# The first experts' second offset: from a TensorE product in PSUM to a GpSimd addition in SBUF

## The chip, the cores and the metric

The kernel runs on one core of a Trainium2 chip. A core has engines with instruction queues of their own that meet only at semaphores: TensorE (PE, products and transposes into PSUM), VectorE (DVE), ScalarE (ACT), GpSimd (POOL) and SyncE (SP, which here only issues DMAs). The metric is device microseconds (us) of one execution, less is better. In the profile PEld stands for TensorE's loading of the stationary operand.

## What is computed

The whole program is four layers on 12,500 nodes of 256 features: a graph layer, a layer of 8 experts, a second graph layer, and attention with 4 experts. The change touches the layer of 8 experts alone:

```python
# L0_ffn, E = 8 experts, C slots for each, D = 256, F = 1024
buf  = zeros((E, C, D)).at[idx, pos_safe].set(x)              # rows sent to their expert
hmid = relu(einsum('ecd,edf->ecf', buf, w1) + b1[:, None, :])
ybuf = einsum('ecf,efd->ecd', hmid, w2) + b2[:, None, :]      # b2: the second offset
```

`b2` has one row of 256 numbers for each expert, added to each row of that expert's result.

## The kernel before

`program` calls one function for each stage, with a barrier of all engines between them. `run_experts` is the stage of the 8 experts. Two jobs that share no data run in it side by side.

**The experts** are TensorE's job. The 8 x 2048 slots are cut into 32 blocks (`NB`) of 512 rows, four blocks for an expert. For block `g` TensorE makes 8 tiles of the hidden layer (`hid_ps`, L1568), each from two products, ScalarE applies ReLU and the first offset to each (L1607), and then TensorE makes four result tiles of 128 x 256 (`y_ps`, index `q`, L1587), each a sum over 8 products in PSUM. Ahead of these 8 stands one product of the first three partitions, `ones_bf` by `b2_bf` (L1583): its three rows are three bf16 parts of `b2` that add up to its float32 value, and it writes the offset to the tile first (`start=True`). ScalarE copies each tile to the buffer `y` in SBUF (L1614, two buffers) and raises `y_done`. SP stores a block when its four tiles are copied (`store`, L1522). Between the result tiles 0 and 2 of a block TensorE also transposes the next block's rows (`turn_rows`, L1550).

**A sort** of edge records is VectorE's job, with help. It is a bitonic network on keys `key` and a payload `pay`, both 128 x 2048 float32. Its steps are `flip` (a change of sign, L374), `swap` (compare and exchange at a distance) and `turn` (a transposition by TensorE). A swap is five instructions of VectorE in a chain, each waiting for the one before: a mask `is_gt` (L384), `min` (L385), `max` (L386), and two predicated copies that move the payload (L390, L391). The first predicated copy overwrites what the second needs, so GpSimd copies half of the payload to `spare` first (`sort_holds`, L404): the copy waits for the step before (`w.chain`), and VectorE waits for the copy (`w.held`) ahead of L390. In this stage run 105 swaps, 14 turns and 7 flips, and GpSimd does nothing but the 105 copies.

In a turn TensorE transposes eight pieces of 128 x 512 (`sort_turn`, L415) and VectorE copies each back from PSUM (L379), so a turn needs both engines at the same time: TensorE waits there for VectorE's chain, VectorE for TensorE's transposes. Where the turns stand in TensorE's queue is fixed by `turn_places`. It counts 6 slots for a block (two in the hidden layer, one behind each result tile, 192 in all), gives each sort step a cost (flip 1, turn 9, swap 7, 868 in all), and places a turn at the slot that the cost spent so far reaches, with `FILL = 0.9` of the slots for the whole sort. The 14 turns stand at slots 0, 8, 20, 30, 42, 54, 65, 78, 90, 104, 116, 132, 144 and 161. Behind the last turn come 7 more swaps.

Ahead of the sort VectorE splits `b2` into its three parts (`split_offsets`, ten instructions on three partitions, L1620 to L1632). When the sort is done VectorE writes the records and counts them, TensorE adds up the counts at the end of the last block's hidden layer (`plan_sums`, L182), VectorE makes the plan's columns of the sums, and SP stores them (`plan_store`, L188) and the last block of results.

Of the kernel before, what the change touches and what calls it, by code (L numbers as in the profile page):

```python
# [5 lines left out]
F32, I32, BF16, U16 = mybir.dt.float32, mybir.dt.int32, mybir.dt.bfloat16, mybir.dt.uint16  # L6
ALU, ACT, AX = mybir.AluOpType, mybir.ActivationFunctionType, mybir.AxisListType

P = 128
N, D = 12500, 256  # L10
# [103 lines left out]
def bc(ap, n, axis=2):  # L114

    a = ap.unsqueeze(axis)
    shape = list(a.shape)
    shape[axis] = n
    return a.to_broadcast(shape)
# [1343 lines left out]
def turn_places(w, first, last, slots):  # L1463


    cost = lambda step, by: {"flip": 1, "turn": 9, "swap": 7}[step]
    total = sum(cost(*w.steps[i]) for i in range(first, last))
    places, spent = {}, 0
    for i in range(first, last):
        if w.steps[i][0] == "turn":  # L1470
            places.setdefault(min(slots - 1, int(spent * FILL / total * slots)), []).append(i)
        spent += cost(*w.steps[i])
    return places


FILL = 0.9


def run_experts(nc, k, xbuf, w1, b1, w2, b2, ybuf, w, first, plan, dest):
# [7 lines left out]
    NB = EXPERTS * BLOCKS  # L1487
    last = len(w.steps)
    with Stage(nc) as s:
        w1s = [s.sb(f"w1s{n}", [P, 2, HID], F32) for n in range(2)]  # L1490
        w2s = [s.sb(f"w2s{n}", [P, FC, D], F32) for n in range(2)]
        b1s = [s.sb(f"b1s{n}", [P, FC], F32) for n in range(2)]
        b2_all, b2_left = s.sb("b2_all", [3, EXPERTS, D], F32), s.sb("b2_left", [3, EXPERTS, D], F32)
        b2_part, b2_bf = s.sb("b2_part", [3, EXPERTS, D], F32), s.sb("b2_bf", [3, EXPERTS, D], BF16)
        ones_bf = s.sb("ones_bf", [3, P], BF16)
        x = [s.sb(f"x{n}", [P, 4, D], F32) for n in range(2)]
        xt = [s.sb(f"xt{n}", [P, 2, W], F32) for n in range(2)]
        hid = [s.sb(f"hid{n}", [P, FC, W], F32) for n in range(2)]
        y = [s.sb(f"y{n}", [P, 4, D], F32) for n in range(2)]
        xt_ps = s.ps("xt_ps", [P, W])  # L1500
        hid_ps = [s.ps(f"hid_ps{n}", [P, W]) for n in range(HB)]
        y_ps = [s.ps(f"y_ps{n}", [P, 512]) for n in range(2)]
        sort_ps = [s.ps(f"sort_ps{h}", [P, 512])[:, :] for h in range(2)]
        r = Records(s, w, plan, sort_ps[0])
        weights, x_loaded, y_stored = ([s.sem(f"{n}{h}") for h in range(2)] for n in ("weights", "x_loaded", "y_stored"))
        turned, xt_done, hid_mult, hid_done, y_mult, y_done, b2_in, split, b2_done = (s.sem(n) for n in (
            "turned", "xt_done", "hid_mult", "hid_done", "y_mult", "y_done", "b2_in", "split", "b2_done"))
        places = turn_places(w, first, last, NB * 6)
        with nc.Block() as block:
            @block.sync  # L1510
            def _(sp):
                def load_weights(e):
                    n = e % 2
                    if e >= 2:
                        sp.wait_ge(y_mult, (e - 1) * BLOCKS * 4)
                    sp.dma_start(w1s[n][:, :, :], w1[e, :, :].rearrange("(c p) f -> p c f", p=P)).then_inc(weights[n], 16)
                    sp.dma_start(w2s[n][:, :, :], w2[e, :, :].rearrange("(c p) d -> p c d", p=P)).then_inc(weights[n], 16)
                    sp.dma_start(b1s[n][:, :], b1[e, :].rearrange("(c p) -> p c", p=P), allow_slow_non_contiguous=True).then_inc(weights[n], 16)

                def store(g):  # L1520
                    sp.wait_ge(y_done, g * 4 + 4)
                    sp.dma_start(yv[g, :, :, :], y[g % 2][:, :, :]).then_inc(y_stored[g % 2], 16)  # L1522

                for g in range(NB):
                    if g >= 2:
                        sp.wait_ge(turned, (g - 1) * 2)
                    sp.dma_start(x[g % 2][:, :, :], xv[g, :, :, :]).then_inc(x_loaded[g % 2], 16)
                    if g == 0:
                        sp.dma_start(b2_all[:, :, :], b2.unsqueeze(0).to_broadcast([3, EXPERTS, D])).then_inc(b2_in, 16)
                        load_weights(0)  # L1530
                    if g % BLOCKS == 1 and g < NB - BLOCKS:
                        load_weights(g // BLOCKS + 1)
                    if g >= 2:
                        store(g - 2)
                store(NB - 2)
                records_stored(sp, w, r, dest)
                store(NB - 1)
                sp.wait_ge(r.columns.kept, 16)
                sp.wait_ge(r.stored, 16)
                for h in range(2):  # L1540
                    sp.wait_ge(y_stored[h], 16 * (NB // 2))

            @block.tensor
            def _(pe):
# [14 lines left out]
                for g in range(NB):  # L1559
                    n, wide = g // BLOCKS % 2, slots_of(g)  # L1560
                    pe.wait_ge(xt_done, g * 2 + 2)
                    pe.wait_ge(weights[n], 48 * (g // BLOCKS // 2 + 1))
                    for fc in range(FC):
                        h = g * FC + fc
                        if h >= HB:
                            pe.wait_ge(hid_done, h - HB + 1)
                        for c in range(2):
                            ins = nc.tensor.matmul(hid_ps[h % HB][:, 0:wide], w1s[n][:, c, fc * P:(fc + 1) * P], xt[g % 2][:, c, 0:wide], start=c == 0, stop=c == 1)  # L1568
                        ins.then_inc(hid_mult, 1)
                        if fc % 4 == 3:  # L1570
                            sort_turns(g * 6 + fc // 4)
                    if g == NB - 1:
                        plan_sums(nc, pe, k, r.columns)
                    for q in range(4):
                        if q % 2 == 0 and g < NB - 1:
                            turn_rows(g + 1, q // 2)
                        m = g * 4 + q
                        if m >= 2:
                            pe.wait_ge(y_done, m - 1)
                        out = y_ps[q % 2][:, 0:D]  # L1580
                        if m == 0:
                            pe.wait_ge(b2_done, 1)
                        nc.tensor.matmul(out, ones_bf[:, :], b2_bf[:, g // BLOCKS, :], start=True, stop=False)  # L1583
                        for fc in range(FC):
                            if q == 0:
                                pe.wait_ge(hid_done, g * FC + fc + 1)
                            ins = nc.tensor.matmul(out, hid[g % 2][:, fc, q * P:(q + 1) * P], w2s[n][:, fc, :], start=False, stop=fc == FC - 1)  # L1587
                        ins.then_inc(y_mult, 1)
                        sort_turns(g * 6 + 2 + q)

            @block.scalar
            def _(act):
# [6 lines left out]
                for g in range(NB):  # L1599
# [8 lines left out]
                    for q in range(4):  # L1608
                        if q % 2 == 0 and g < NB - 1:
                            copy_turned(g + 1, q // 2)  # L1610
                        act.wait_ge(y_mult, g * 4 + q + 1)
                        if q == 0 and g >= 2:
                            act.wait_ge(y_stored[g % 2], 16 * (g // 2))
                        nc.scalar.activation(y[g % 2][:, q, :], y_ps[q % 2][:, 0:D], ACT.Copy).then_inc(y_done, 1)  # L1614

            @block.vector
            def _(dve):
                def split_offsets(link):

                    link(nc.vector.memset(ones_bf[:, :], 1.0))  # L1620
                    dve.wait_ge(b2_in, 16)
                    for row in range(3):
                        own = k.ident[0:3, row:row + 1]
                        link(nc.vector.tensor_scalar(b2_left[:, :, :].bitcast(I32), b2_all[:, :, :].bitcast(I32), 16, 16,
                                                     ALU.logical_shift_right, ALU.logical_shift_left))
                        if row < 2:
                            link(nc.vector.tensor_tensor(b2_all[:, :, :], b2_all[:, :, :], b2_left[:, :, :], ALU.subtract))
                        if row == 0:
                            link(nc.vector.tensor_scalar(b2_part[:, :, :], b2_left[:, :, :], own, None, ALU.mult))
                        else:  # L1630
                            link(nc.vector.scalar_tensor_tensor(b2_part[:, :, :], b2_left[:, :, :], own, b2_part[:, :, :], ALU.mult, ALU.add))
                    link(nc.vector.tensor_copy(b2_bf[:, :, :], b2_part[:, :, :]))  # L1632
                    dve.sem_inc(b2_done, 1)

                split_offsets(Chain(dve, split))
                sort_on_vector(nc, dve, w, first, last, sort_ps)
                records_on_vector(nc, dve, k, w, r)

            @block.gpsimd
            def _(pool):  # L1640
                sort_holds(pool, nc.gpsimd.tensor_copy, w, first, last)


def normalize_nodes(nc, k, sums, params, x_old, x_left, f_turned, w, width, result):
# [852 lines left out]
```

## Time and profile before

| | us |
|---|---|
| median of 3 runs | 9306.64 |
| lowest and highest | 9304.74, 9342.89 |
| the profiled execution, its own time | 9387.91 |
| its span, first to last instruction | 9386.1 |

| in the profiled execution | |
|---|---|
| the stage `run_experts` | 2775 to 3843 us |
| PE busy, whole span | 5874.7 us (63%) |
| POOL busy | 4973.1 us (53%) |
| DVE busy | 4494.3 us (48%) |
| ACT busy | 3781.8 us (40%) |

The shares over the whole span are means over ten stages with different limits. What the change is worth has to be read in its stage, from four views: the busy times of the engines in stretches, the groups of instructions by line, the waits, and the instructions in order of time. The profiled execution is 81 us longer than the median; the difference is not in one stage's rows, and its own durations are used against its own span.

### The profile page before, as it was taken

Reading aid. Unit: us, or ns where it says so; the run is one execution under the profiler, and the core shown is the slowest. Engines: PE = TensorE matmul, PEld = TensorE weight load, DVE = VectorE, ACT = ScalarE, POOL = GpSimd, SP = SyncE. Lnnn points to the kernel's source line nnn. Section 1 sums busy time; section 2 is a strip of 40 time slices with the busy share of each in tenths; the row PEclk is TensorE's granted clock in tenths of the full one; section 3 lists DMA queues with packets and bytes.
Section 4 is the critical chain, followed back from the end, with each engine's and each line's share of the span. In section 5 each row is a group of like instructions: output and inputs, shape, how many; then the busy total and the mean of one; then the engine's idle time right before and its main releaser. Section 6 shows DMA issues by size and latency. Waiting matters only on the chain. (4 is left out here: it accounts for less than half of the span.)

```text
span 9386.1 us, 89224 instructions
## 1 busy us (share of the span) xinstructions
PE 5874.7 (63%) x19881; PEld 3964.3 (42%) x19881; DVE 4494.3 (48%) x8790; ACT 3781.8 (40%) x9693; POOL 4973.1 (53%) x4762
## 2 busy tenths in 40 slices
PE   5455555555569999655555555555647677676755
PEld 4333333333356666333443333333624444444444
DVE  4444555545569999564544444444711111111125
ACT  5555555555552222444554554555401111111113
POOL 4666666666542222546666666666454544454532
PEclk8666667777659999876776676676568878787878
DMA  5333333333321111542332222232321111111126
GB/s 147 99 99 100 98 100 101 95 90 89 100 97 41 50 54 41 142 150 87 89 89 84 86 83 83 84 89 81 130 56 43 41 41 41 42 42 42 44 74 253
DMA packets 500454, 797.42 MB, mean 85 GB/s; under 512 B 123070, under 2 KB 365355, under 8 KB 499851
## 3 DMA queue, kind: packets, MB, share of 16 engines
q0 software_dynamic: 200256, 453.47, 18.0%
q1 hardware_dynamic: 299696, 338.23, 11.2%
q8 instruction: 196, 3.21, 0.1%
q14 instruction: 306, 2.51, 0.1%
HBM read 595.60 MB, written 197.30 MB: 84 GB/s over the span
## 5 line engine op out<-in xcount | busy, mean ns | idle before, releaser
L1017 PE MATMUL part<-rows,spread 128*128 x6656 | 2441.4, 523 | 2142.5 <-issue 1124.7
L1017 PEld LDWEIGHTS part<-rows,spread 128*128 128x128 f32 x6656 | 1624.7, 261 | 2905.8 <-issue 2631.6
L974 DVE TENSOR_TENSOR agg<-agg,part 128x257 f32 (+1 forms) x3328 | 1405.6, 422 | 2401.1 <-issue 866.3
L957 POOL DMA_INDIRECT rows<-h,row x1563 | 1555.7, 995 | 876.9 <-issue 439.9
L957 POOL DMA_INDIRECT rows<-f,row x1563 | 1555.2, 995 | 767.3 <-issue 456.8
L1041 ACT ACTIVATE spread<-iota,place 128x128 f32<-128x128 f32 x3328 | 1020.2, 392 | 2186.2 <-PE part L1017 1057.9
L1921 POOL DMA_INDIRECT rows<-gat,src x1122 | 1062.0, 947 | 1097.4 <-DVEq L2108 764.5
L1996 PE MATMUL y_ps<-agg,hid 128*128 128x256 f32 x3136 | 888.0, 423 | 658.4 <-issue 653.1
L1996 PEld LDWEIGHTS y_ps<-agg,hid 128*128 128x128 f32 x3136 | 661.1, 212 | 906.0 <-issue 821.1
L1047 ACT ACTIVATE spread<-spread,weight 128x128 f32<-128x128 f32 x3328 | 1021.2, 391 | 14.5 <-ACT spread L1043 0.9
L2126 DVE TENSOR_TENSOR y_all<-y_ps,b 128x512 f32<-128x512 f32 x196 | 135.5, 692 | 1792.1 <-DMA h<-res 1046.2
L2029 ACT ACTIVATE hid<-hid_ps,b 128x512 f32<-128x512 f32 (+1 forms) x400 | 261.5, 679 | 1684.8 <-DMA own<-sorted_e 1214.1
L1985 PE MATMUL hid_ps<-agg,w 128*128 128x512 f32 (+1 forms) x1600 | 707.9, 594 | 40.3 <-issue 28.3
L404 POOL COPY spare<-pay 128x1024 f32<-128x1024 f32 x105 | 222.5, 2119 | 735.3 <-DVE pay L391 505.6
L1043 ACT ACTIVATE spread<-spread,ones 128x1024 f32<-128x1024 f32 x416 | 478.6, 1150 | 38.9 <-remote 21.3
L1587 PE MATMUL y_ps<-w2s,hid 128*128 128x256 f32 x2048 | 476.2, 386 | 0.0
L1985 PEld LDWEIGHTS hid_ps<-agg,w 128*128 128x128 f32 x1600 | 312.0, 195 | 382.7 <-issue 356.3
L1568 PE MATMUL hid_ps<-xt,w1s 128*128 128x512 f32 (+1 forms) x1024 | 427.7, 574 | 3.5 <-DMA b1s<-in_L_ffn_b 3.5
L385 DVE TENSOR_TENSOR key<-key 128x1024 f32<-128x1024 f32 (+1 forms) x342 | 414.1, 1211 | 6.1
L1587 PEld LDWEIGHTS y_ps<-w2s,hid 128*128 128x128 f32 x2048 | 378.5, 190 | 61.7
L386 DVE TENSOR_TENSOR key<-key 128x1024 f32<-128x1024 f32 (+1 forms) x342 | 337.5, 987 | 11.8
L1607 ACT ACTIVATE hid<-hid_ps,b1s 128x512 f32<-128x512 f32 (+1 forms) x256 | 171.2, 669 | 329.0 <-PE hid_ps L1568 329.0
(393 smaller groups left out, 6035.2 us busy)
## 6 DMA issues: line engine op xcount, KB each, us to landing
expert_rows<-y_all SPq DMA_DIRECT2D x196, 256.0 KB
made<-expert_rows SPq DMA_DIRECT2D x49, 1024.0 KB
x<-x SPq DMA_DIRECT2D x42, 896.0 KB
rows<-f,row POOLq DMA_INDIRECT x1563
rows<-h,row POOLq DMA_INDIRECT x1563
rows<-gat,src POOLq DMA_INDIRECT x1122
xbuf<-zero SPq DMA_DIRECT2D x128, 128.0 KB
x<-xbuf SPq DMA_DIRECT2D x32, 512.0 KB
```

Of the source, the lines that this page charges most:

```text
L385: link(nc.vector.tensor_tensor(b[:, :, 0, :], a[:, :, 0, :], a[:, :, 1, :], ALU.min))
L957: pool.indirect_dma_start(out=rows[:, u, 0:D], out_offset=None, in_=table, in_offset=bass.IndirectOffsetOnAxis(ap=q.row[:, i:i + 1], axis= ...
L974: nc.vector.tensor_tensor(sum_t, sum_t, part[:, p % NB, 0:WIDE], ALU.add).then_inc(added, 1)
L1017: nc.tensor.matmul(part[:, p % NB, 0:WIDE], spread[:, p % (2 * BANKS), :], row_p, start=True, stop=True).then_inc(multiplied, 1)
L1041: nc.scalar.activation(spread[:, p % (2 * BANKS), :], k.iota[:, :], ACT.Square, bias=q.place[:, p:p + 1]).then_inc(squared, 1)
L1043: nc.scalar.activation(spread[:, h, :], spread[:, h, :], ACT.Relu, scale=-1.0, bias=k.ones[:, 0:1]).then_inc(marked, 1)
L1047: nc.scalar.activation(spread[:, p % (2 * BANKS), :], spread[:, p % (2 * BANKS), :], ACT.Copy, scale=q.weight[:, p:p + 1]).then_inc(spread ...
L1568: ins = nc.tensor.matmul(hid_ps[h % HB][:, 0:wide], w1s[n][:, c, fc * P:(fc + 1) * P], xt[g % 2][:, c, 0:wide], start=c == 0, stop=c == 1)
L1587: ins = nc.tensor.matmul(out, hid[g % 2][:, fc, q * P:(q + 1) * P], w2s[n][:, fc, :], start=False, stop=fc == FC - 1)
L1921: pool.indirect_dma_start(out=rows[b % 3][:, j, :], out_offset=None, in_=table, in_offset=at(src[:, b * B + j:b * B + j + 1])).then_inc(ga ...
L1985: ins = nc.tensor.matmul(hid_ps[m % HB][:, 0:cols_n], w1[:, e, d, fc * P:(fc + 1) * P], ft[n // GEXP % 2][:, d, 0:cols_n], start=d == 0, s ...
L1996: ins = nc.tensor.matmul(y_ps[m % 2][:, q, :], hid[n % 2][:, fc, at:at + P], w2[:, n % GEXP, fc, :], start=fc == 0, stop=fc == FC - 1)
```

## The change

GpSimd adds the offset, to the four result tiles of a block at once, in SBUF. In full:

- `b2` is loaded for all 128 partitions (`b2_p`, 128 x 8 x 256 float32) in the place of the load for three partitions, in the same place of SP's queue, ahead of the first weights. The split into three parts on VectorE goes, and with it `ones_bf`, `b2_bf` and `b2_done`.
- The product L1583 goes, 128 of them. The first of the 8 products of a tile starts the sum.
- GpSimd's `add(g)` waits until the four tiles of block `g` are copied and adds the expert's row to 128 x 1024 numbers, in place. There are 32 such additions. `turn_places` returns for each step of the sort the slot it reaches (`reached`), and `add(g)` stands ahead of the first payload copy whose step reaches slot `(g + 1) * 6`; four are left behind the last copy.
- The store of a block waits for its addition (`offset`) in the place of `y_done`.
- `y` has four buffers in the place of two.

```diff
@@ run_experts
-        b2_all, b2_left = s.sb("b2_all", [3, EXPERTS, D], F32), s.sb("b2_left", [3, EXPERTS, D], F32)
-        b2_part, b2_bf = s.sb("b2_part", [3, EXPERTS, D], F32), s.sb("b2_bf", [3, EXPERTS, D], BF16)
-        ones_bf = s.sb("ones_bf", [3, P], BF16)
+        b2_p = s.sb("b2_p", [P, EXPERTS, D], F32)
+        YB = 4
...
@@ sync
-                    sp.wait_ge(y_done, g * 4 + 4)
-                    sp.dma_start(yv[g, :, :, :], y[g % 2][:, :, :]).then_inc(y_stored[g % 2], 16)
+                    sp.wait_ge(offset, g + 1)
+                    sp.dma_start(yv[g, :, :, :], y[g % YB][:, :, :]).then_inc(y_stored[g % YB], 16)
...
-                        sp.dma_start(b2_all[:, :, :], b2.unsqueeze(0).to_broadcast([3, EXPERTS, D])).then_inc(b2_in, 16)
+                        sp.dma_start(b2_p[:, :, :], b2.unsqueeze(0).to_broadcast([P, EXPERTS, D])).then_inc(b2_in, 16)
@@ tensor
-                        if m == 0:
-                            pe.wait_ge(b2_done, 1)
-                        nc.tensor.matmul(out, ones_bf[:, :], b2_bf[:, g // BLOCKS, :], start=True, stop=False)
...
-                            ins = nc.tensor.matmul(out, hid[g % 2][:, fc, q * P:(q + 1) * P], w2s[n][:, fc, :], start=False, stop=fc == FC - 1)
+                            ins = nc.tensor.matmul(out, hid[g % 2][:, fc, q * P:(q + 1) * P], w2s[n][:, fc, :], start=fc == 0, stop=fc == FC - 1)
@@ vector
-                split_offsets(Chain(dve, split))
@@ gpsimd
-                sort_holds(pool, nc.gpsimd.tensor_copy, w, first, last)
+                def add(g):
+                    pool.wait_ge(y_done, g * 4 + 4)
+                    rows = y[g % YB][:, :, :]
+                    nc.gpsimd.tensor_tensor(rows, rows, bc(b2_p[:, g // BLOCKS, :], 4, 1), ALU.add).then_inc(offset, 1)
+
+                pool.wait_ge(b2_in, 16)
+                g = 0
+                for i in range(first, last):
+                    while g < NB - 1 and (g + 1) * 6 <= reached[i]:
+                        add(g)
+                        g += 1
+                    sort_holds(pool, nc.gpsimd.tensor_copy, w, i, i + 1)
+                for g in range(g, NB):
+                    add(g)
```

On GpSimd, at the start of `run_experts` (L404 is the payload copy, L1624 the addition):

```order
-L1639 UNCONDITIONAL_BRANCH
-L404 COPY spare<-pay 128x1024 x105
-L1509 UNCONDITIONAL_BRANCH
+L1619 UNCONDITIONAL_BRANCH
+L404 COPY spare<-pay 128x1024 x3
+L1624 TENSOR_TENSOR y_57979<-y_57979,b_p 128x1024
+L404 COPY spare<-pay 128x1024 x3
+L1624 TENSOR_TENSOR y_57980<-y_57980,b_p 128x1024
+L404 COPY spare<-pay 128x1024 x5
+L1624 TENSOR_TENSOR y_57981<-y_57981,b_p 128x1024
+L404 COPY spare<-pay 128x1024 x3
```

The one unbroken row of 105 copies is cut: an addition stands behind every three to five copies, 28 in all, and four more behind the last copy.

On TensorE, the first block's result tiles, before:

```order
L1568 MATMUL hid_ps_57987<-xt_57979,w1s_57966 128x512 x2
L1550 MATMUL xt_ps<-ident,x_57978 128x128 x4
L1583 MATMUL y_ps_57989<-b_bf,ones_bf 128x256
L1587 MATMUL y_ps_57989<-w2s_57968,hid_57981 128x256 x8
L1583 MATMUL y_ps_57990<-b_bf,ones_bf 128x256
L1587 MATMUL y_ps_57990<-w2s_57968,hid_57981 128x256 x8
L1550 MATMUL xt_ps<-ident,x_57978 128x128 x4
```

and with the change:

```order
L1569 MATMUL hid_ps_57985<-xt_57975,w1s_57966 128x512 x2
L1551 MATMUL xt_ps<-ident,x_57974 128x128 x4
L1585 MATMUL y_ps_57987<-w2s_57968,hid_57977 128x256 x8
L1585 MATMUL y_ps_57988<-w2s_57968,hid_57977 128x256 x8
L1551 MATMUL xt_ps<-ident,x_57974 128x128 x4
```

Only the product L1583 ahead of each result tile is gone. The order of all that remains, the turns' slots among it, is the same.

## Rows read from the trace of the kernel before

**Rows 1.** Busy time by stretch (us, PE, PEld, DVE, ACT, POOL, granted clock, DMA):

```profile
2900.00:3000.00 100.00, 98.25 (x388) 64.16 (x387) 95.15 (x72) 24.16 (x42) 23.24 (x11) 1.00 0.16 53
...
3154.00:3161.00 7.00, 6.59 (x30) 5.11 (x29) 4.62 (x7) 0.00 (x0) 0.00 (x0) 0.51 0.06 22
```

**Rows 2.** Waits of the stage (who, for whom: us in total, times, longest):

```profile
DVE first L209 <- PE sort_ps L182: 58.5, 1, 58.5
DVE key L379 <- PE sort_ps L415: 24.9, 16, 3.7
...
PE sort_ps L415 <- DVE key L374: 6.2, 2, 3.7
```

**Rows 3.** Groups by line and shape, the stage (busy us, mean ns, idle before):

```profile
L404 POOL COPY spare<-pay 128x1024 f32<-128x1024 f32 x105 | 222.5, 2119 | 735.3 <-DVE pay L391 505.6 <-DVE pay L379 229.6
L385 DVE TENSOR_TENSOR key<-key 128x1024 f32<-128x1024 f32 x105 | 206.3, 1964 | 3.6
...
L391 DVE COPY_PREDICATED pay<-mask,spare 128x1024 f32<-128x1024 uint16 x105 | 167.1, 1591 | 3.6
...
L384 DVE TENSOR_TENSOR mask<-key 128x1024 uint16<-128x1024 f32 x105 | 128.7, 1225 | 3.6
...
L1583 PE MATMUL y_ps<-b_bf,ones_bf 3*128 3x256 bf16 x128 | 35.5, 278 | 0.0
...
L374 DVE TENSOR_SCALAR key<-key,sign 128x2048 f32<-128x2048 f32 x7 | 9.0, 1286 | 0.4
```

**Rows 4.** Order of time, TensorE's result tiles in the last blocks (start, us, engine):

```profile
3753.51 0.28 PE L1583 MATMUL y_ps<-b_bf,ones_bf 3*128 3x256 bf16 x1
...
3753.72 3.72 PE L1587 MATMUL y_ps<-w2s,hid 128*128 128x256 f32 x16
...
3757.37 0.28 PE L1583 MATMUL y_ps<-b_bf,ones_bf 3*128 3x256 bf16 x1
```

**Rows 5.** The line of `min`, L385, in an earlier stage, 300 to 2700 us:

```profile
L385 DVE TENSOR_TENSOR key<-key x66: 1224/1225/1229, 312.7 to 2538.7; 128x1024 f32<-128x1024 f32 x66
```

**Rows 6.** Order of time, VectorE and GpSimd in a later stage:

```profile
6644.89 3.95 POOL L1713 TENSOR_TENSOR part<-agg,gain 128x1792 f32<-128x1792 f32 x1
...
6646.19 4.53 DVE L1818 SCALAR_TENSOR_TENSOR agg<-part,x 128x1792 f32<-128x1792 f32 x1 [0.22 <-DVE mv L1824]
6648.92 5.62 POOL L1715 TENSOR_TENSOR part<-part,beta_p 128x1792 f32<-128x1792 f32 x1
```

**Rows 7.** Groups by line and shape, GpSimd over the whole span:

```profile
L721 POOL TENSOR_TENSOR agg<-agg,b 128x1792 f32<-128x1792 f32 x14 | 51.3, 3679 | 51.4 <-ACT f L775 47.2 <-issue 4.2
```

**Rows 8.** Order of time, TensorE: first products, first turn, last turn, sums of the counts:

```profile
2785.55 8.75 PE L1568 MATMUL hid_ps<-xt,w1s 128*128 128x512 f32 x16 [3.50 <-DMA b1s<-in_L_ffn_b]
...
2796.76 1.09 PE L415 MATMUL sort_ps<-ident,key 128*128 128x128 f32 x8 [2.45 <-DVE key L374]
...
3667.74 1.09 PE L415 MATMUL sort_ps<-ident,key 128*128 128x128 f32 x8 [1.08 <-DVE pay L391]
...
3802.41 0.50 PE L182 MATMUL sort_ps<-cnt,ones 98*128 98x198 f32 x2
```

**Rows 9.** Order of time, two turns, first and last piece of each:

```profile
3153.51 1.46 PE L415 MATMUL sort_ps<-ident,key 128*128 128x128 f32 x8 [3.71 <-DVE key L374]
...
3160.53 1.44 DVE L379 COPY pay<-sort_ps 128x512 f32<-128x512 f32 x2 [0.42 <-PE sort_ps L415]
...
3225.47 1.04 PE L415 MATMUL sort_ps<-ident,key 128*128 128x128 f32 x8
...
3229.20 2.92 DVE L379 COPY pay<-sort_ps 128x512 f32<-128x512 f32 x4
```

**Rows 10.** Order of time, SP: the last store, and the next stage's first load:

```profile
3818.80 5.63 SPq L1522 DMA_DIRECT2D ybuf<-y  x1
3842.60 0.97 SPq L1306 DMA_DIRECT2D x<-x  x2
```

More of the change, by code:

```diff
@@ L1467, in turn_places @@
     total = sum(cost(*w.steps[i]) for i in range(first, last))
-    places, spent = {}, 0
+    places, reached, spent = {}, {}, 0
     for i in range(first, last):
+        reached[i] = min(slots - 1, int(spent * FILL / total * slots))
         if w.steps[i][0] == "turn":
-            places.setdefault(min(slots - 1, int(spent * FILL / total * slots)), []).append(i)
+            places.setdefault(reached[i], []).append(i)
         spent += cost(*w.steps[i])
-    return places
+    return places, reached
 FILL = 0.9
@@ L1498, in run_experts @@
         hid = [s.sb(f"hid{n}", [P, FC, W], F32) for n in range(2)]
-        y = [s.sb(f"y{n}", [P, 4, D], F32) for n in range(2)]
+        y = [s.sb(f"y{n}", [P, 4, D], F32) for n in range(YB)]
         xt_ps = s.ps("xt_ps", [P, W])
@@ L1504, in run_experts @@
         r = Records(s, w, plan, sort_ps[0])
[L1505 to L1508, printed above, removed]
+        weights, x_loaded = ([s.sem(f"{n}{h}") for h in range(2)] for n in ("weights", "x_loaded"))
+        y_stored = [s.sem(f"y_stored{h}") for h in range(YB)]
+        turned, xt_done, hid_mult, hid_done, y_mult, y_done, b2_in, offset = (s.sem(n) for n in (
+            "turned", "xt_done", "hid_mult", "hid_done", "y_mult", "y_done", "b2_in", "offset"))
+        places, reached = turn_places(w, first, last, NB * 6)
         with nc.Block() as block:
@@ L1539, in _ @@
                 sp.wait_ge(r.stored, 16)
-                for h in range(2):
-                    sp.wait_ge(y_stored[h], 16 * (NB // 2))
+                for h in range(YB):
+                    sp.wait_ge(y_stored[h], 16 * (NB // YB))
             @block.tensor
@@ L1611, in _ @@
                         act.wait_ge(y_mult, g * 4 + q + 1)
-                        if q == 0 and g >= 2:
-                            act.wait_ge(y_stored[g % 2], 16 * (g // 2))
-                        nc.scalar.activation(y[g % 2][:, q, :], y_ps[q % 2][:, 0:D], ACT.Copy).then_inc(y_done, 1)
+                        if q == 0 and g >= YB:
+                            act.wait_ge(y_stored[g % YB], 16 * (g // YB))
+                        nc.scalar.activation(y[g % YB][:, q, :], y_ps[q % 2][:, 0:D], ACT.Copy).then_inc(y_done, 1)
             @block.vector
             def _(dve):
[L1618 to L1633, printed above, removed]
-                split_offsets(Chain(dve, split))
                 sort_on_vector(nc, dve, w, first, last, sort_ps)
```

## The prediction

> **What bounds the kernel now.** The change lies in one stage of some 1068 us of a span of 9386.1, so I read that stage alone. First the busy times by stretch [rows 1]: in 100 us of it TensorE is busy for 98.25 and VectorE for 95.15, while GpSimd has 23.24. Two engines are full at once, and that is the point of the case: what leaves TensorE helps only as far as VectorE can follow. Next the waits [rows 2]. At the turns VectorE waits for TensorE's transposes for 24.9 us in 16 waits, and TensorE waits for VectorE hardly at all, 6.2 us in two. So TensorE sets the pace, but VectorE is close behind it.
>
> How close, from the groups [rows 3]. A swap is five chained instructions: L384 and L386 at 1.23 us each (one row stands for both), L385 at 1.96, L390 and L391 at 1.59 each, and five gaps of 3.6/105 = 0.034: 7.77 us. Between the first turn and the last lie 98 of the 105 swaps, 761 us, and 6 flips at 1.3 us, 8 us. A turn takes 6.65 us from TensorE's first transpose (3225.47) to the end of VectorE's last copy (3229.20 + 2.92) [rows 9]; 13 of them with one slower one are 88 us. VectorE's chain is 857 us. The two engines took 3667.74 - 2796.76 = 871 us for it [rows 8]. VectorE's slack is 14 us, 1.6%. The same number comes from the waits: in a turn 0.8 us pass before VectorE's eight copies begin (6.65 - 2 x 2.92), the first transposes, which no order of work saves. That is 11 for 14 turns, and of the 24.9 us 14 are left. After the last turn VectorE has plenty: it waits 58.5 us for the sums of the counts [rows 2].
>
> **What the change removes.** On TensorE, 128 products L1583. From the start of one to the start of the sum behind it pass 0.21 us, and from there to the next such product 3.65 [rows 4]. The 16 records of a sum take 3.72 us with the last one's 0.38 in it, so they start 0.22 apart and 16 starts are 3.56: of a tile's 3.86 us at least 0.21 and some 0.30 go; if the weight loads then run on without a gap, up to 0.43. I take 0.32: 41 us over 128 tiles, if TensorE went on to set the pace. The last turn stands behind 27 blocks: 108 of the tiles, 35 us, are ahead of it, and 16 between it and the sums of the counts, 5 us.
>
> On VectorE the split of the offsets goes. It ran ahead of the sort, and TensorE had waited 2.45 us for the first flip when it began the first turn at 2796.76 [rows 8]. So without the split the first turn could come 2.5 us sooner. But the load of the offsets grows from 24 KB to 1 MB and stands ahead of the weights for which TensorE's first product waits until 2785.55 [rows 8]. The queue moved 2.5 MB in the 10.5 us from the stage's begin at 2775, so 1 MB is worth at most 4 us. The two cancel to within 2 us: I set the first turn at 2797 as before.
>
> **What it adds.** An addition on 128 x 1024 numbers, in place, with one operand repeated for each tile. The nearest row is of the same form on 1792 columns, 3.68 us [rows 7]: 2.10 us by the columns. The product of the later stage took 3.95 [rows 6]: 2.26. I take 2.2, with 2.1 and 2.3 as ends. GpSimd has room for 32 of them many times over. What counts is whom it holds up.
>
> That the trace shows twice. L385 takes 1.224 us in a stage where GpSimd copies nothing [rows 5], and 1.96 here [rows 3]; L384, when the copy was just begun, is not slowed, and the copy takes 2.12 us, of which L384's 1.23 lie in front. So the copy waits for L384 and then L385 waits for the copy. In the later stage it stands in the open [rows 6]: GpSimd's L1713 ends at 6648.84, VectorE's L1818 begun at 6646.19 ends at 6650.72, 1.88 us behind it, and L1715 issued at 6648.92 takes 5.62 in the place of about 3.95. They take turns, a whole instruction at a time. An addition that follows a payload copy therefore begins when L385 ends, and L386 waits for all of its 2.2 us.
>
> The Trainium skill says this in SBUF — State Buffer, section Who interferes with whom: the shared port pair is an exclusive lock for the whole instruction, and a VectorE instruction with two SBUF inputs contends with a GpSimd one that reads SBUF. The rows agree. By that rule the predicated copies, with mask and data from SBUF, block too, which no row here shows. GPSIMD Engine Reference, section 3.1, gives 4497 ns for an addition of 2048 columns; half of it would be 2.25 us and the same sum.
>
> Of the 28 additions between copies 26 stand ahead of the last turn (slot 161 has passed 26 blocks' ends): 26 x 2.2 = 57 us on VectorE's chain. Two things change it. GpSimd reaches an addition right after a copy, up to 8 us before VectorE reaches the step that it was placed ahead of. Where TensorE has not ended the block by then, GpSimd waits for it. Some two additions then fall into a turn, where VectorE reads PSUM and blocks nobody (-4). Two or three others keep the next payload copy waiting behind them until L390 needs it, 3 us each at most (+6).
>
> **The sum.** VectorE's chain from first to last turn: 857 + 57 - 4 + 6 = 916 us, against TensorE's 871 - 35 = 836. VectorE is now the bound, by far. The last turn comes at 2797 + 916 = 3713, 45 us later than at 3667.74. From there to the sums of the counts TensorE runs freely, 134.7 us before [rows 8], 5 less now: +40. Behind the sums come the plan's columns and its store, unchanged. The last block's addition delays the last store by 2.2 us. That store's issue alone took 5.63 us, since the plan's small pieces filled the queue, and the next stage began 24 us after the last tile [rows 10]: I cost it at nothing, at most 2. The additions behind the last copy fall into the 58.5 us. SP's store of a block waits for the addition now, with the next load of rows behind it, which has some 20 us to spare.
>
> **A second price, of the clock.** TensorE will wait at the turns for 45 + 35 + its present 7 = 87 us, 6.7 us at each of 13. One wait of 3.71 us stands in the trace: it ended at 3153.51, and in the 7 us from 3154 on the granted clock is 0.51, the lower level of 1.2 GHz, against 1.00 around it [rows 1, 9]. After a wait of 2.45 us the transposes ran at full speed (1.09 us for eight, against 1.46) [rows 8, 9]. The slow turn took 3160.53 + 1.44 - 3153.51 = 8.46 us in the place of 6.65, 1.8 more, and a turn is VectorE's time as well. If ten of the thirteen turns come slow, that is 18 us. TensorE's own work at the lower clock is covered by its waits.
>
> Together +58 with predicated copies that block, +51 if an addition beside one costs nothing (some additions start late, in that part of a swap). I take +54. Profiled span 9386 + 54 = 9440; on the median, 9306.6 + 54 = 9361 us, ratio 1.0058.
>
> **The rivals.**
> - The clock stays up, since the transposes of a turn and the tiles around it keep it. For it: only one fall in this stage. Against: that one came at the shortest wait of those I expect. Then +36 (33 to 43): 9343.
> - The additions do not hold VectorE, for instance because they land in gaps or in turns. This ends on the other side. Even with all of them free VectorE's chain stays at 857 us, so the last turn gains 14 at the most and the tail 5: -17, 9290. It decides below 0.65 us per addition on VectorE: 26 x 0.65 = 17, the slack of 14 with the tail's 5, less 2 for the waits. Against: rows 5 and 6. It also shows that the whole 41 us of TensorE's gain is out of reach.
> - GpSimd waits for `y_done` with the payload copy behind it at most additions, not at two or three. It decides once TensorE is late against the plan of slots, which the slow clock could bring about. Price: up to 3 us at ten more, 30 us: +84, 9391.
>
> **How the numbers follow.** What a measurement here can tell from no change is about 0.5%, 46.5 us. The forecast case has 0.60; it spans +40 to +66, and 0.48 of it I put above 46.5, 0.12 below. The clock that stays has 0.18 (within), free additions 0.08 (within), waits for `y_done` 0.11 (slower), and 0.03 are left for a gain that I don't see. Slower 0.59, within 0.38, faster 0.03. The range leaves the free additions out: low end 2.1 us each, no slow clock, no blocking by predicated copies, 0.43 saved per tile, +18: 9325. High end 2.3 us each, all turns slow, and waits for the payload copy at most additions, +85: 9392.
>
> **What the next profile would show.** L386 at the 28 steps at about 3.4 us, its mean up from 1.23 to some 1.8; L385 as before; the addition's group 32 times at 2.1 to 3.5 us with VectorE's rest in front. VectorE's wait L379 <- L415 down to some 10 us plus the slower transposes, TensorE's waits for L374 and L391 in L415 up to some 80. Granted clock below 1.00 in most stretches with a turn. The last turn at about 3725 to 3735, the sums of the counts at about 3855. It is wrong if L386 stays at 1.23, if the addition runs beside it, or if TensorE still does not wait at the turns.

## The result and the profile after

The changed kernel is slower: 9367.4 us against 9306.0, ratio (this kernel's time by the time before) 1.0066 with a 95% interval of 1.0053 to 1.0078. The forecast was 9361 us. In a second comparison the ratio was 1.0056 (1.0043 to 1.0069).

The spans of the two profiled executions (9386.1 before, 9372.8 after) don't show this, since stages that the change doesn't touch differ between them by 66 us. The stage does: from SP's first load to the next stage's first gather it took 1068.2 us before (2775.1 to 3843.3) and 1120.8 after (2755.3 to 3876.1), 52.6 more; in the second comparison's profile it took 1121.5. That is the number to explain. Of the 61 us between the medians some 9 are in no row of the stage; 52.6 us of 9306 are 0.57%, which lies inside both intervals.

Busy time by stretch, as in [rows 1] (the second stretch lies over a turn's wait):

```profile
2900.00:3000.00 100.00, 93.08 (x350) 62.87 (x349) 95.47 (x65) 24.35 (x42) 33.64 (x15) 0.97 0.16 53
3148.00:3161.00 13.00, 5.81 (x24) 4.42 (x24) 10.45 (x9) 0.00 (x0) 0.00 (x0) 0.50 0.25 81
```

TensorE fell from 98.25 to 93.08 busy in 100 us, while VectorE is as full as before. The waits of the stage, as in [rows 2]:

```profile
POOL y L1624 <- ACT y L1612: 130.8, 19, 26.1
...
DVE first L209 <- PE sort_ps L182: 48.0, 1, 48.0
PE sort_ps L415 <- DVE pay L391: 47.7, 7, 12.0
...
DVE key L379 <- PE sort_ps L415: 45.8, 47, 21.2
PE sort_ps L415 <- DVE key L374: 42.7, 6, 11.0
...
DVE pay L390 <- POOL spare L404: 6.6, 2, 3.3
```

TensorE's waits for VectorE at the turns grew from 7 to 90 us (47.7 + 42.7), over 13 turns. VectorE's own 45.8 us look like more than the 24.9 of before, but 21.2 of them are the first turn, for which VectorE is ready early now that it has nothing to split. The other 24.6 are the first transposes of each turn and the slower transposes of the slow ones. And the groups, as in [rows 3]:

```profile
L385 DVE TENSOR_TENSOR key<-key 128x1024 f32<-128x1024 f32 x105 | 204.9, 1952 | 3.6
...
L390 DVE COPY_PREDICATED pay<-mask,pay 128x1024 f32<-128x1024 uint16 x105 | 172.9, 1647 | 10.1 <-POOL spare L404 6.6
L391 DVE COPY_PREDICATED pay<-mask,spare 128x1024 f32<-128x1024 uint16 x105 | 171.0, 1629 | 3.6
L386 DVE TENSOR_TENSOR key<-key 128x1024 f32<-128x1024 f32 x105 | 163.2, 1555 | 3.6
L384 DVE TENSOR_TENSOR mask<-key 128x1024 uint16<-128x1024 f32 x105 | 138.7, 1321 | 3.6
...
L1624 POOL TENSOR_TENSOR y<-y,b_p 128x1024 f32<-128x1024 f32 x32 | 92.2, 2881 | 130.8 <-ACT y L1612 130.8
```

Against before L386 has 34.6 us more, L384 10.0, L390 6.1, L391 3.9, L385 1.4 less, and L390 waited 6.6 us for payload copies: 59.8 us on VectorE, by nothing but the additions. Instruction by instruction against the trace of before, 17 of the 28 additions between copies fell on L386, five on L384, three on L390 and one on L391, and each of these took 2.0 to 2.2 us more. The other two held no instruction, but the payload copy behind them came late, and L390 waited 3.3 us each time. Ahead of the last turn stand 27 of the 28: 49.5 us of longer instructions and the 6.6 of waiting, 56.1 in all. One of them in the order of time (start, us, engine, line; GpSimd and VectorE):

```profile
2869.29 2.18 POOL L404 COPY spare<-pay 128x1024 f32<-128x1024 f32 x1 [4.98 <-DVE pay L391]
2871.43 3.32 POOL L1624 TENSOR_TENSOR y<-y,b_p 128x1024 f32<-128x1024 f32 x1
...
2870.52 2.03 DVE L385 TENSOR_TENSOR key<-key 128x1024 f32<-128x1024 f32 x1
2872.58 3.25 DVE L386 TENSOR_TENSOR key<-key 128x1024 f32<-128x1024 f32 x1
```

The addition was issued at 2871.43, when L385 had just got its turn; it ran only from L385's end at 2872.55 on, 2.2 us, and L386 took 3.25 in the place of 1.23, 2.02 more. A second one came late, since GpSimd had waited for its block:

```profile
3325.33 2.35 POOL L1624 TENSOR_TENSOR y<-y,b_p 128x1024 f32<-128x1024 f32 x1 [3.64 <-ACT y L1612]
3325.37 3.44 DVE L391 COPY_PREDICATED pay<-mask,spare 128x1024 f32<-128x1024 uint16 x1
```

Here it began 0.04 us ahead of a predicated copy, which took 3.44 us in the place of about 1.3. So predicated copies are held as well, which no row of before had shown.

The turns, as in [rows 8, 9]: the last one, and TensorE's result tiles in an earlier stretch of the same trace:

```profile
3703.62 3.94 PE L415 MATMUL sort_ps<-ident,key 128*128 128x128 f32 x16 [11.97 <-DVE pay L391]
...
2993.65 0.60 PE L1551 MATMUL xt_ps<-ident,x 128*128 128x128 f32 x4
2994.08 7.07 PE L1585 MATMUL y_ps<-w2s,hid 128*128 128x256 f32 x32
3000.99 0.60 PE L1551 MATMUL xt_ps<-ident,x 128*128 128x128 f32 x4
```

The second and third of these rows show what was won: two result tiles take 6.91 us (2994.08 to 3000.99). Before it was 0.21 + 3.65 for each [rows 4], and 0.54 from the transposes to the product against 0.43 now. A block of 30.05 us became one of 28.42, 0.41 us less a tile. The first row shows how it was lost again: 12 us of waiting at one turn.

### The profile page after: what moved, and what is told of

The parts are those of the page before. It is cut to its first block and busy times, and to the rows that moved or that the text cites. A ratio compares the mean times of both kernels' runs of the same rounds, so it can differ in the third digit from the quotient of the medians.

```text
span 9372.8 us, 89019 instructions
## 1 busy us (share of the span) xinstructions
PE 5881.9 (63%) x19753; PEld 3988.9 (43%) x19753; DVE 4534.8 (48%) x8780; ACT 3772.1 (40%) x9693; POOL 5049.8 (54%) x4794
## 5 line engine op out<-in xcount | busy, mean ns | idle before, releaser
L1017 PE MATMUL part<-rows,spread 128*128 x6656 | 2476.7, 529 | 2038.5 <-issue 1135.4
L404 POOL COPY spare<-pay 128x1024 f32<-128x1024 f32 x105 | 219.8, 2094 | 663.7 <-DVE pay L391 445.0
L1585 PE MATMUL y_ps<-w2s,hid 128*128 128x256 f32 x2048 | 453.1, 379 | 0.0
L385 DVE TENSOR_TENSOR key<-key 128x1024 f32<-128x1024 f32 (+1 forms) x342 | 412.8, 1207 | 6.1
L386 DVE TENSOR_TENSOR key<-key 128x1024 f32<-128x1024 f32 (+1 forms) x342 | 372.2, 1088 | 11.8
```

The source lines that it names most:

```text
L385: link(nc.vector.tensor_tensor(b[:, :, 0, :], a[:, :, 0, :], a[:, :, 1, :], ALU.min))
L1017: nc.tensor.matmul(part[:, p % NB, 0:WIDE], spread[:, p % (2 * BANKS), :], row_p, start=True, stop=True).then_inc(multiplied, 1)
```

## The experiments

My theory: an addition on GpSimd and a VectorE instruction that reads two operands from SBUF take turns, so each addition lengthens VectorE's chain (the expectations say by 2.16 us, which was the longest L386; 2.03 is the usual price, as e2 shows); that chain had 14 us of slack, is now the bound up to the last turn, and the clock falls when TensorE waits for it. The rivals: the new waits of the results' path cost the time, or the addition does harm wherever it stands, or the price sits on TensorE or the loads.

The kernels ran on three chips, each beside the kernel before, which took 7774 us (e1 to e4), 9385 (e5 to e8) and 7779 (e9, e10) there. Nearly all of that difference lies outside this stage (some 6705 or 8320 us). No kernel was profiled on chips of both kinds, so that the stage is equal on them is not shown directly; but its difference from the 1068.2 us of before agrees in each of these ten runs to about 6 us or better with the difference of the medians on its own chip. So I compare stages directly, and ratios only on one chip. For each run, in us: from the first turn's transposes to the last turn's, from there to the sums of the counts, TensorE's waits of over 1 us ahead of turns (the first turn's among them), the sum of turns 3 to 14 from first transpose to VectorE's last copy, and the whole stage. Turns 1 and 2 took 6.65 to 6.72 us in every run.

| run | ratio (95%) | to last turn | to sums | waits | turns | stage |
|---|---|---|---|---|---|---|
| before | 1 | 871.0 | 134.7 | 7.2 | 82.0 | 1068.2 |
| the change | 1.0066 (1.0053 to 1.0078) | 926.4 | 129.2 | 90.4 | 95.6 | 1120.8 |
| e1_small_add | 0.9988 (0.9979 to 0.9997) | 864.5 | 129.5 | 35.4 | 88.5 | 1055.5 |
| e2_scratch_adds | 1.0065 (1.0051 to 1.0079) | 921.2 | 136.2 | 46.1 | 92.2 | 1119.5 |
| e3_adds_in_turns | 0.9992 (0.9983 to 1.0001) | 865.0 | 129.5 | 34.0 | 90.1 | 1058.6 |
| e4_fill95 | 1.0008 (0.9999 to 1.0017) | 923.9 | 85.5 | 50.3 | 89.7 | 1073.2 |
| e5_change_again | 1.0056 (1.0043 to 1.0069) | 926.6 | 129.2 | 90.3 | 95.9 | 1121.5 |
| e6_turns_fill95 | 0.9963 (0.9948 to 0.9977) | 882.2 | 84.6 | 13.8 | 84.5 | 1031.8 |
| e7_filler | 1.0041 (1.0026 to 1.0055) | 918.8 | 129.1 | 33.9 | 87.5 | 1112.9 |
| e8_no_offset_fill95 | 0.9965 (0.9951 to 0.9978) | 881.9 | 84.6 | 13.9 | 84.2 | 1026.5 |
| e9_before_fill95 | 0.9988 (0.9979 to 0.9997) | 909.8 | 89.0 | 1.7 | 80.4 | 1062.8 |
| e10_turns_fill965 | 0.9952 (0.9939 to 0.9966) | 885.1 | 83.1 | 10.4 | 83.6 | 1031.6 |

### e1_small_add: the additions made small

```diff
-                    rows = y[g % YB][:, :, :]
-                    nc.gpsimd.tensor_tensor(rows, rows, bc(b2_p[:, g // BLOCKS, :], 4, 1), ALU.add).then_inc(offset, 1)
+                    rows = y[g % YB][:, :, 0:8]
+                    nc.gpsimd.tensor_tensor(rows, rows, bc(b2_p[:, g // BLOCKS, 0:8], 4, 1), ALU.add).then_inc(offset, 1)
```

> The changed kernel with GpSimd's additions cut to 8 of the 256 columns of each tile (the other columns of the results lack their offset); all waits, stores, the load and the places are as in the change. Theory, additions hold VectorE: an addition on 32 columns holds it for some 0.1 us, so VectorE's chain between first and last turn falls from the changed kernel's 926 us to about 860, L386's mean goes back from 1.555 to about 1.23 us, and the kernel comes out some 17 us below the kernel before, ratio 0.998. Rival, the new waits (GpSimd waits for y_done with a payload copy behind it, the store waits for the addition): these are all still there, so the ratio stays near 1.006.

The loss is gone, with every wait and store of the change still in place. The group of L386 in the stage of this run:

```profile
L386 DVE TENSOR_TENSOR key<-key 128x1024 f32<-128x1024 f32 x105 | 128.7, 1226 | 3.6
```

That is before's 128.6. The new waits are no cause. But the stage is 12.7 us shorter than before, not 17 as the theory had it, and the chain to the last turn takes 864.5 us, not about 860. The row of the table says why: TensorE, faster now, still waits 35 us at the turns, and the turns are 6.5 us slower than before's. Less these it is 858 us, the chain that was counted.

### e2_scratch_adds: additions alone, in the kernel before

```diff
+                nc.gpsimd.memset(extra[:, :, :], 0.0).then_inc(zeroed, 1)
+                nc.gpsimd.memset(row[:, :], 0.0).then_inc(zeroed, 1)
+                g = 0
+                for i in range(first, last):
+                    while g < NB - 1 and (g + 1) * 6 <= reached[i]:
+                        pool.wait_ge(zeroed, g + 2)
+                        nc.gpsimd.tensor_tensor(extra[:, :, :], extra[:, :, :], bc(row[:, :], 4, 1), ALU.add).then_inc(zeroed, 1)
+                        g += 1
+                    sort_holds(pool, nc.gpsimd.tensor_copy, w, i, i + 1)
```

> The kernel before, with its products and its split kept, and 28 additions of 128 x 1024 on a buffer of their own put on GpSimd at the places of the change; they wait for nothing of the experts. Theory, additions hold VectorE: 26 x 2.16 = 56 us on its chain, less its slack of 14, so +42, and TensorE waits some 4 us at each turn, at some of which the clock falls (+5 to +10): ratio 1.005. Rival, the loss comes of the results' path (waits for y_done, later stores): nothing of it is here, ratio 1.000.

Additions that nobody waits for, in a kernel that keeps its products, cost as much as the whole change: 51 us. Their group and L386's:

```profile
L386 DVE TENSOR_TENSOR key<-key 128x1024 f32<-128x1024 f32 x105 | 185.5, 1767 | 3.6
L1650 POOL TENSOR_TENSOR extra<-extra,extra_row 128x1024 f32<-128x1024 f32 x28 | 93.0, 3321 | 0.0
```

All 28 follow a payload copy at once, so all fall on L386: 185.5 - 128.6 = 56.9 us, 2.03 each. In the trace 27 of them, not the expected 26, stand ahead of the last turn: 54.6 us; less before's slack of 14, with 10 us of slower turns, that is 51, and the time to the last turn grew by 50. The rival of the results' path is excluded from this side too.

### e3_adds_in_turns: the same additions where VectorE reads PSUM

```diff
-                    while g < NB - 1 and (g + 1) * 6 <= reached[i]:
-                        add(g)
-                        g += 1
+                    if w.steps[i][0] == "turn" and (g + 1) * 6 <= reached[i] + 1:
+                        pool.wait_ge(w.chain, w.links[i])
+                        while (g + 1) * 6 <= reached[i] + 1:
+                            add(g)
+                            g += 1
```

The six buffers (`YB = 6`) and the stores four blocks behind, `store(g - 4)`, are needed since a block may now wait for its turn for nearly three blocks.

> The changed kernel with the same 32 full additions, but GpSimd makes them when VectorE's chain has reached a turn (27 of them in 13 turns, 5 behind the last copy); six result buffers and stores two blocks later. Theory, additions hold VectorE only beside instructions that read two operands from SBUF: in a turn VectorE reads PSUM, so the additions take 2.2 to 2.3 us and cost nothing, VectorE's chain is back at 857 to 862 us, and the ratio is 0.998 (17 us below before). Rival, any GpSimd work, or its reading and writing in SBUF, slows VectorE or the results wherever it stands: L379's mean rises above 0.69 us and the ratio stays above 1.003.

```profile
L386 DVE TENSOR_TENSOR key<-key 128x1024 f32<-128x1024 f32 x105 | 130.7, 1245 | 3.6
L1625 POOL TENSOR_TENSOR y<-y,b_p 128x1024 f32<-128x1024 f32 x32 | 75.6, 2382 | 166.3 <-ACT y L1613 78.5 <-DVE key L374 52.2 <-DVE pay L391 35.6
...
L379 DVE COPY pay<-sort_ps 128x512 f32<-128x512 f32 x56 | 38.7, 692 | 6.2 <-PE sort_ps L415 3.2 <-DVE pay L379 0.4
```

The additions take 2.38 us in the place of 2.88, and L379, beside which they run, keeps its 692 ns to the nanosecond. So an addition is harmless beside this VectorE copy that reads PSUM, and the chain (865.0) is that of e1. No long instruction is left ahead of the last turn; the two additions that still hold the sort stand behind it. The "only two operands from SBUF" of my theory is too narrow, though: beside the last block's addition the conversion L233, with one operand in SBUF, took 1.91 us in the place of 0.17. The mechanism held but for this; the gain was smaller than expected, 9.6 us of the stage, for e1's reason and since the last block's addition now stands in the way of the end (below).

### e4_fill95: the turns later in TensorE's queue

```diff
-FILL = 0.9
+FILL = 0.95
```

> The changed kernel with FILL = 0.95 in the place of 0.9: the turns stand later in TensorE's queue, the last at slot 170 instead of 161, so nine slots, some 43 us, of TensorE's work move from behind the last turn to before it. Theory, VectorE's chain is the bound up to the last turn and TensorE waits there: the chain stays near 920 us, the last turn comes no later, what follows it is 43 us shorter, and TensorE's waits at the turns fall from 6.7 to 3.4 us, so that fewer turns are slow: 43 to 53 us below the changed kernel, ratio 1.001 to 1.002. Rival, the loss sits on TensorE or on the loads (a price for each block): the places change nothing, ratio 1.0066.

The last turn came no later although TensorE had nine slots more to do ahead of it (923.9 us against 926.4), and what follows took 85.5 us against 129.2. TensorE's waits fell to 50 us and eight turns were slow, not twelve. So up to the last turn TensorE was not the bound. The stage is 48 us shorter than the change's, as expected.

### e5_change_again

> The changed kernel as it is, beside the others of this call on one chip, so that they can be compared with it. Its stage is some 52 us longer than before in the two traces; ratio 1.0066 to 1.007.

The stage and each of its parts repeat to within a microsecond.

### e7_filler: TensorE kept busy at the turns

```diff
+                fillers = dict(zip(sorted(i for own in places.values() for i in own), [0, 0, 5, 5, 3, 2, 10, 4, 3, 6, 5, 7, 5, 11]))
...
+                        if fillers[i]:
+                            pe.wait_ge(w.chain, w.links[max(j for own in places.values() for j in own if j < i) + 1])
+                        for _ in range(fillers[i]):
+                            nc.tensor.matmul(sort_ps[0], k.ident[:, :], xt[slot // 6 % 2][:, 0, :], start=True, stop=True)
```

> The changed kernel with products of 128 x 512 whose result nobody reads put ahead of each turn on TensorE (0.86 us each, none to eleven, cut to the wait less 2 us that its trace shows at that turn), so that TensorE is not idle there. VectorE's additions stay as they are. Theory, the lower clock in the turns costs the changed kernel 13 to 15 us: the clock stays at 1.00, the turns take 6.7 instead of 7.9 us, and the kernel is 13 us faster than the changed one, ratio 1.005. Rival, the slow turns are only a sign of the waits and VectorE would lose the same time anyway: no change against the changed kernel, 1.0068.

The stage is 8.6 us shorter than the change's, all of it in the turns (95.9 to 87.5), with VectorE's groups unchanged. The two ratios, 1.0041 and 1.0056, point the same way, but their intervals overlap; it is the profile that carries this. I had expected 13 us. The fillers left waits of 2.4 to 2.9 us, and in eight of the twelve turns behind them the clock fell all the same. Two turns (TensorE's first transposes):

```profile
3189.82 3.77 PE L415 MATMUL sort_ps<-ident,key 128*128 128x128 f32 x16 [2.46 <-DVE key L374]
...
3412.69 1.09 PE L415 MATMUL sort_ps<-ident,key 128*128 128x128 f32 x8 [2.72 <-DVE pay L391]
```

After 2.46 us of waiting sixteen transposes took 3.77 us and the whole turn 7.92; after 2.72 us, a longer wait, eight took 1.09 and the turn 6.70, at full clock.

### e6_turns_fill95 and e8_no_offset_fill95: what there is to win

e6 has the diffs of e3 and of e4. e8 is the kernel before less these:

```diff
-                        if m == 0:
-                            pe.wait_ge(b2_done, 1)
-                        nc.tensor.matmul(out, ones_bf[:, :], b2_bf[:, g // BLOCKS, :], start=True, stop=False)
...
-                split_offsets(Chain(dve, split))
...
-FILL = 0.9
+FILL = 0.95
```

> Additions in the turns, as in e3_adds_in_turns, and FILL = 0.95 as in e4_fill95. Theory, VectorE's chain of 857 us was what kept TensorE's saving out of the total: with nine more slots ahead of the last turn TensorE has 836 + 43 = 879 us to that turn and is the bound again, waits there little, and its full saving of about 41 us shows: ratio 0.995 (40 us below before), last turn to the sums of the counts 86 us. Rival, the saving on TensorE is smaller than 0.32 us a tile, or there is nothing to win once the turns lie elsewhere: ratio 0.998 to 1.000.

> The kernel before without the second offset (neither its load, its split nor its products; the results lack it), with FILL = 0.95. It gives what can be won at most by taking the offset from TensorE: 0.32 us a tile by the sum, 41 us, and the weights are not delayed. Theory: ratio 0.9945, with 0.30 to 0.43 us a tile gone between the result tiles. If the weight loads keep the pace of the tiles, it is 0.21 us a tile and the ratio is 0.9965.

Both medians lie 0.4% below before, with 1.0 outside the intervals: with the additions where they hold nobody and the turns where VectorE can follow, the change becomes a gain of 36 us of the stage, and leaving the offset out altogether gives 42. Both ratios missed the theory's, 0.995 and 0.9945. That of e8 is the very one of its rival, 0.21 us a tile, but not by the rival's reason: a block takes 28.42 us in both runs' traces against 30.05, so the saving on TensorE is 0.41 us a tile, 52 us in all, more than I took. TensorE still waited 14 us at the turns, and five and four turns were slow; that is where part of the rest is seen.

### e9_before_fill95 and e10_turns_fill965: a control and a step further

Nothing but `FILL`: 0.95 in the kernel before, 0.965 in e6.

> Control: the kernel before with nothing but FILL = 0.95. Before the change TensorE sets the pace up to the last turn and behind it, so moving its turns moves none of its work out: ratio 0.998 to 1.001. If this alone gave 0.996, the gain of e6_turns_fill95 would be the places' and not the offset's.

> Additions in the turns with FILL = 0.965 (last turn at slot 172 or 173 instead of 170). In e6_turns_fill95 TensorE still waited 1.5 to 2.7 us at seven turns, 14 us in all, and five turns were slow. With more of its work ahead of each turn these waits shrink: up to 10 us less than e6, ratio 0.9955. Against it: behind the last turn TensorE has some 75 us left and VectorE needs 70 (7 swaps and the records), so nothing more is to be had beyond this.

In the kernel before the later turns bring 5 us of the stage: TensorE's last waits at turns go (7.2 to 1.7 us). So of e6's 36 us of the stage about 31 are the offset's; by the ratios, 0.9963 against 0.9988 with the intervals just apart, it is 0.25% or 23 us. e10 has the best ratio, 0.9952, but it stands against the median of another chip, and its stage (1031.6) equals e6's (1031.8): the 10 us that I expected are not there. TensorE waited less at the turns and in exchange for VectorE's counts behind the sort (DVEq is VectorE's queue):

```profile
PE sort_ps L182 <- DVEq L200: 5.6, 1, 5.6
PE sort_ps L415 <- DVE pay L391: 5.2, 3, 1.9
PE sort_ps L415 <- DVE key L374: 5.2, 2, 2.6
```

## Why the prediction was right

**The slack of 14 us.** It carried everything, and it held: 26 additions at 2.2 us were set against it. e1 and e3 show the chain without them, e2 with them alone. e4 shows which engine it is that waits.

**The price of an addition.** Forecast 2.2 us on VectorE. Measured 2.03, in all 28 cases of e2 and in nearly all of the changed kernel; only where the addition began a few hundredths of a microsecond ahead of the VectorE instruction did it lose more, at most 2.18. The addition scaled from 1792 columns of another stage [rows 7] was thus 8% too dear. The count was one too small: GpSimd makes an addition right behind the copy ahead of its place, so that 27 and not 26 stand ahead of the last turn. That predicated copies are held too, on which the sum left 7 us open, is settled: five of them were held, and took 3.3 to 4.3 us. L386's mean rose to 1.555 us and not to the 1.8 forecast, since GpSimd waited for its block at 15 of the 28 additions and at most of these met another instruction of the swap.

**The additions in turns and the copies behind waiting ones.** Forecast 4 us less for two additions in turns: ahead of the last turn there was none. Forecast +6 for two or three late payload copies: measured 6.6 us at two places. The rival of waits for `y_done` at most additions was thus right on the waits and wrong on their price: most ended before VectorE needed the copy.

**The clock.** Right in kind, wrong in size and number: twelve turns were slow, not ten, by 1.3 us on average over 6.65 and not by the 1.8 of the one slow turn in the trace of before [rows 9]. That is 15.8 us; the one slow turn was already in the 857 us of before, so 13.6 are new, where the forecast added 18 and so counted it twice. A single row had been taken for the mean; with waits of 4 to 12 us the clock was back up before the turn's end in several turns. e7 took 8.4 us of it away.

**TensorE's saving.** Mis-sized: 0.32 us a tile taken, 0.41 measured. The upper end named, 0.43 if the weight loads run on without a gap, was nearly the truth. It cost the forecast little, as only 16 of the 128 tiles stand where TensorE sets the pace.

**The sum.** To the last turn forecast 916 us and 18 for the clock, 934; measured 926.4, of which 13.6 for the clock. To the sums forecast 129.7; measured 129.2. TensorE's waits forecast 87 us; measured 90.4. The first turn stood 21.7 us behind the stage's begin before and 21.8 now: no gain from the split, as forecast, since the larger load took it back. e8, with neither split nor load, has it at 19.3.

**Luck in the total.** The forecast had two branches, +58 us if predicated copies are held and +51 if not, and took +54. They are held, so the branch that applied is +58, and the stage measured +52.6: the chain and the clock came 7.6 us lower than forecast, the end 2.4 higher. That +54 lies so near owes something to the branch that turned out wrong.

**What failed.** The end, from the sums of the counts to the next stage, was costed at nothing, at most 2 us, and took 2.4. The last block's addition ran from 3847.65 for 2.34 us, while VectorE still made the plan's columns. It held the last of them, the conversion L233, here before and after:

```profile
3817.67 0.17 DVE L233 CAST tint<-lcol 128x2 int32<-128x2 f32 x1
...
3847.65 2.34 POOL L1624 TENSOR_TENSOR y<-y,b_p 128x1024 f32<-128x1024 f32 x1 [23.03 <-ACT y L1612]
3847.82 0.26 DVE L232 TENSOR_REDUCE lcol<-sel 128x1 f32<-128x99 f32 x1
3848.12 1.90 DVE L233 CAST tint<-lcol 128x2 int32<-128x2 f32 x1
3850.10 0.38 SPq L188 DMA_DIRECT2D plan_e<-tint  x1
3850.53 6.27 SPq L1523 DMA_DIRECT2D ybuf<-y  x1
```

So the plan's store slipped from 15.5 to 17.3 us behind the sums, and the last store behind it from 16.4 to 17.7. The same 1.9 us of L233 stand in every run whose last full addition lies there, and 0.17 in the five others. Of the 2.4 us these are 1.3. The other 1.1 lie between the last store and the next stage's gather, which took 24.5 us before and 25.6 in the changed kernel, but also 25.6 in e9, whose end is that of before: they are no more than what varies. I had looked only at the store behind the addition (covered, as said), not at who reads SBUF beside it.

And the rival of free additions was priced at -17 us; e1 and e3 gave -13 and -10. Its sum allowed 2 us for TensorE's waits; TensorE, being faster, waited 35 and 34 us at the turns even then, and the price in clock made the turns 6.5 and 8.1 us slower.

**Open.** Why the medians differ by 61 us where the stage differs by 53. The second comparison, 54 us between medians at the same stage time, speaks for chance, but I did not test it. Nor did I place the turns by measured durations in the place of `turn_places`' costs, which might win some of the 14 us of waits left in e6.

## What to carry to other kernels

Before work is taken from a full engine, work out the slack of the next one in the same stage, here 14 us in 871: as long as the places where the two meet stay, that caps the gain up to the last of them, whatever the first engine saves. An elementwise instruction of GpSimd is not free because GpSimd is idle. Here each addition cost VectorE 2.0 us of the 2.34 that it takes, beside instructions with two operands in SBUF, and nothing beside copies from PSUM, so it was put there. Not every instruction with one operand in SBUF is safe: the conversion L233 was held, the reduction L232 was not, and others were not tried. When the bound moves to the other engine, positions laid out for the old one have to move with it.

## What the runs showed of the hardware that I had not expected

- VectorE's predicated copy of 128 x 1024 took 3.44 us beside a GpSimd addition that began 0.04 us before it, against about 1.3.
- VectorE's copies from PSUM keep 692 ns for 128 x 512 with a GpSimd addition beside them and without; the addition takes 2.38 us there.
- A conversion of 128 x 2 from float32 to int32, with one operand in SBUF, took 1.90 us beside a GpSimd addition in the place of 0.17, while a reduction of 128 x 99 kept its 0.26 us beside the same addition.
- After waits of TensorE of 2.4 to 2.9 us the granted clock fell in some turns and not in others, and not by length (in e7 a fall at 2.46 us, none at 2.72; in e1 a fall within a turn already after 1.38); in the changed kernel, after waits of 4.4 us and more, it was low for part of all twelve turns.
